# A pre-norm decoder layer with mixture of experts: the first half's order of steps laid out anew

## The reference

```
x = x + attn(ln(x))        # latent attention: down to 32 channels, rotary, causal softmax
                           # within the tile, back to 256
x = x + xattn(ln(x), ctx)  # 32 query heads in 8 groups, head size 8, causal softmax
x = x + ffn(ln(x))         # 32 experts, inner size 96, gated by silu;
                           # the best 8 by softmax, kept until their share reaches 0.8
```

## Time and profile before

| | |
|---|---|
| median of 3 runs | 587.49 us |
| lowest, highest | 585.48, 590.56 us |
| the profiled execution | 586.84 us |
| its span, first to last instruction | 584.1 us |
| TensorE busy | 481.9 us (82%) |
| VectorE busy | 380.1 us (65%) |
| GpSimd busy | 326.2 us (56%) |
| ScalarE busy | 310.5 us (53%) |
| granted TensorE clock, mean | 0.956 |

### The profile page before, as it was taken

One profiled execution on the slowest core, in us unless ns is written; L12 is line 12 of the kernel. 1 busy time (PEld: TensorE's weight loads), 2 busy tenths in 40 slices (PEclk: granted clock), 3 DMA queues, 4 the chain that ended last, 5 costly groups with the idle time before them and its releaser, 6 DMA issues.

```text
span 584.1 us, 12942 instructions
## 1 busy us (share of the span) xinstructions
PE 481.9 (82%) x3248; PEld 401.4 (69%) x3248; DVE 380.1 (65%) x1856; ACT 310.5 (53%) x869; POOL 326.2 (56%) x473
## 2 busy tenths in 40 slices
PE   3689999999999999997588688878888888888750
PEld 2577777777787777776377577777777777778640
DVE  4357888787777778787257344444444446978875
ACT  2477777777777777772424234444444444444430
POOL 4112377766666676765555755555555555655570
PEclk9999999999999999997889879999999999999975
DMA  7422448622223223112643667775544569898665
GB/s 206 130 91 81 145 142 242 182 89 94 92 93 103 92 93 103 66 65 88 189 138 128 218 198 251 238 214 159 148 122 131 159 184 291 296 300 281 203 194 186
DMA packets 52408, 93.82 MB, mean 161 GB/s; under 512 B 9991, under 2 KB 41263, under 8 KB 52147
## 3 DMA queue, kind: packets, MB, share of 16 engines
q1 hardware_dynamic: 37346, 46.11, 27.3%
q0 software_dynamic: 12240, 32.14, 14.8%
q10 hardware_dynamic: 2752, 14.76, 8.0%
HBM read 53.61 MB, written 43.41 MB: 166 GB/s over the span
## 4 chain that ended last, share of the span: by engine, by line
PE 59%; issue 11%; DVE 9%; ACT 9%; another core or an unknown queue 7%; DMA 2%; POOL 1%; ACTq 1%; POOLq 0%; DVEq 0%
PE bank L1387 12%; PE bank L1415 10%; PE bank L1087 6%; PE bank L1254 4%; PE bank L1228 4%; PE bank L1342 3%; DVE NM L776 3%; PE bank L1272 3%; PE bank L1267 3%; ACT VC L491 3%; PE bank L1209 2%; DVE NM L778 2%; PE bank L1405 2%; PE bank L1082 2%
## 5 line engine op out<-in xcount | busy, mean ns | idle before, releaser
L466 POOL DMA_INDIRECT rows<-rowb,idx x112 | 110.8, 989 | 65.7 <-DVE rowb L876 36.0
L1415 PE MATMUL bank<-wd_sb,VC 96*128 x286 | 80.9, 406 | 45.5 <-ACT VC L491 38.9
L1387 PE MATMUL bank<-wgu_sb,PT 128*128 x572 | 108.3, 333 | 5.9 <-issue 5.8
L474 POOL DMA_INDIRECT parts<-PT,dst_all x72 | 71.0, 986 | 68.9 <-ACT PT L491 50.9
L1387 PEld LDWEIGHTS bank<-wgu_sb,PT 128*128 128x128 f32 x572 | 93.6, 194 | 7.1 <-issue 7.1
L1415 PEld LDWEIGHTS bank<-wd_sb,VC 96*128 96x128 f32 x286 | 51.3, 195 | 61.6 <-issue 57.1
L985 DVE SCALAR_TENSOR_TENSOR PT<-PT,bank 128x192 f32<-128x192 f32 x72 | 25.2, 350 | 103.5 <-ACT PT L619 73.4
L491 ACT ACTIVATE PT<-bank 128x512 f32<-128x512 f32 (+1 forms) x108 | 64.1, 595 | 36.5 <-remote 13.7
L619 ACT ACTIVATE PT<-bank 128x192 f32<-128x192 f32 x72 | 24.1, 334 | 97.9 <-PE bank L1387 69.0
L585 ACT ACTIVATE PT<-bank 128x512 f32<-128x512 f32 x96 | 53.7, 621 | 4.7 <-PE bank L1254 4.7
L491 ACT ACTIVATE Q<-bank 9x256 fp32r<-9x256 f32 (+1 forms) x96 | 42.8, 446 | 10.2 <-PE bank L1223 6.4
(11 more groups left out here) (270 smaller groups left out, 1166.1 us busy)
## 6 DMA issues: line engine op xcount, KB each, us to landing
pool_a<-rows SPq DMA_DIRECT2D x96, 148.5 KB
qN<-rows SPq DMA_DIRECT2D x47, 148.5 KB
wgu_sb<-wgu_d SPq DMA_DIRECT2D x8, 768.0 KB
rows<-pad SPq DMA_DIRECT2D x33, 152.0 KB
pool_a<-parts ACTq DMA_DIRECT2D x5, 896.0 KB
KA<-parts ACTq DMA_DIRECT2D x5, 896.0 KB
Q<-parts ACTq DMA_DIRECT2D x4, 896.0 KB
wd_sb<-wd_d SPq DMA_DIRECT2D x2, 1536.0 KB
```

The costliest lines, as they stand in the source:

```text
L466: gp.indirect_dma_start(out=rows, out_offset=bass.IndirectOffsetOnAxis(ap=idx[b % 2][:, k:k + 1], axis=0), in_=rowb[b % 2][:, :], in_offse ...
L474: gp.indirect_dma_start(out=parts, out_offset=bass.IndirectOffsetOnAxis(ap=dst[q % NDST][:, j:j + 1], axis=0), in_=yb[q % FEED][:, j, :], ...
L1387: last = t.matmul(GU_PS[q % 2][:, j * 2 * NI:(j + 1) * 2 * NI], xTb[q % 2][:, j, k * P:(k + 1) * P], wgu_sb[:, k, one_of(expert[i]), :].sq ...
L1415: last = t.matmul(Y_PS[q % 2][:, j * D:(j + 1) * D], hTb[q % 2][:, j, :], wd_sb[:, one_of(expert[2 * q + j]), :].squeeze(1), start=True, s ...
```

## The change

All offsets of the first half are replaced, on all engines, and `mx` gets its wait for `Q2` by halves. Cut to its core:

```diff
 PERIOD = 18.74
 AT = {
...
-    "POOL": {"r1": -12, "r4": -2.2, "r7": 3.9, "r13": 17.4, "kL": 29.5, "r17": 46.3, "wo": 51.5, "xT": 60, "sc0": 74.6, "sc1": 77.4, "sc2": 80.5,
-           "sc3": 82.6, "sc4": 84.5, "sc5": 86.4, "sc6": 87.7},
-    "SP": {"ldx": -6.0, "ldc": -2.0, "n3": 42.5, **{f"w{n}": 25.0 + 12.0 * n for n in range(10)}}}
+    "POOL": {"r1": -4.76, "r4": -3.71, "r7": 9.29, "r13": 18.36, "kL": 31.5, "r17": 47, "xT": 50.53, "wo": 52.71, "sc0": 74.6, "sc1": 77.4,
+           "sc2": 80.5, "sc3": 82.6, "sc4": 84.5, "sc5": 86.4, "sc6": 87.7},
+    "SP": {"ldx": -6, "ldc": -2, "n3": 41.27, **{f"w{n}": 25.0 + 12.0 * n for n in range(10)}}}
...
-PAIR0, PAIR = 47.1, 3.2
...
 END = {
-    "PE": {"oT": 46.9, "wo": 50.1, "xT": 53.3, "lg": 56.5, "rk": 59.7},
-    "ACT": {"oT": 47.3, "xT": 53.6, "g1": 57},
...
-    "POOL": {"r17": 28.5, "wo": 51.3}}
+    "PE": {"oT": 49.29, "wo": 49.66, "xT": 51.34, "lg": 51.56, "rk": 57.28},
+    "ACT": {"oT": 45.1, "xT": 51.2, "g1": 57.99},
...
+    "POOL": {"r17": 28.31, "wo": 47.99}}
...
@@ def mx(u)
                     if u == 0:
                         pe.wait_ge(S["KA"], nth("KA", b))
-                        pe.wait_ge(S["Q2"], nth("Q2", b, 2))
+                    if pair == 0:
+                        pe.wait_ge(S["Q2"], nth("Q2", b, hf + 1))
```

More of the change, by code:

```diff
@@ L51 @@
 AT = {
[3 rows of a table removed]
-           "vt": 43.5, "oT": 46.6, "wo": 50.8, "xT": 56.9, "lg": 58.0, "rk": 62.9, "la1": 74.5 + (SEEN - 1) * PERIOD,
-           "la2": 80 + (SEEN - 1) * PERIOD, "la3": 86.2 + (SEEN - 1) * PERIOD},
[6 rows of a table removed]
-           "po": 62.9, "g7": 64, "g8": 73.7, "g9": 74.2, "g10": 75.2, "g11": 75.4, "g12": 75.6, "g13": 75.8, "la1": 77.4 + (SEEN - 1) * PERIOD,
-           "la2": 83 + (SEEN - 1) * PERIOD, "la3": 86.5 + (SEEN - 1) * PERIOD},
-    "POOL": {"r1": -12, "r4": -2.2, "r7": 3.9, "r13": 17.4, "kL": 29.5, "r17": 46.3, "wo": 51.5, "xT": 60, "sc0": 74.6, "sc1": 77.4, "sc2": 80.5,
-           "sc3": 82.6, "sc4": 84.5, "sc5": 86.4, "sc6": 87.7},
@@ L67 @@
-    "SP": {"ldx": -6.0, "ldc": -2.0, "n3": 42.5, **{f"w{n}": 25.0 + 12.0 * n for n in range(10)}}}
[3 rows of a table added]
+           "pv1": 38.53, "vt": 43.63, "oT": 45.66, "wo": 49.31, "xT": 55.7, "lg": 56.09, "rk": 62.4, "la1": 74.5 + (SEEN - 1) * PERIOD,
+           "la2": 80.0 + (SEEN - 1) * PERIOD, "la3": 86.2 + (SEEN - 1) * PERIOD},
[6 rows of a table added]
+           "g9": 73.62, "g10": 74.22, "g11": 74.82, "g12": 75.08, "g13": 75.1, "la1": 77.4 + (SEEN - 1) * PERIOD, "la2": 83.0 + (SEEN - 1) * PERIOD,
+           "la3": 86.5 + (SEEN - 1) * PERIOD},
@@ L71 @@
 END = {
-    "PE": {"oT": 46.9, "wo": 50.1, "xT": 53.3, "lg": 56.5, "rk": 59.7},
-    "ACT": {"oT": 47.3, "xT": 53.6, "g1": 57},
-    "DVE": {"wo": 50.6, "n3": 52.2, "g1": 56.9, "g2": 57.9, "g3": 58, "g4": 58.1, "g5": 58.2, "po": 60.3, "g6": 61, "g7": 61.1},
-    "POOL": {"r17": 28.5, "wo": 51.3}}
+    "PE": {"oT": 49.29, "wo": 49.66, "xT": 51.34, "lg": 51.56, "rk": 57.28},
+    "ACT": {"oT": 45.1, "xT": 51.2, "g1": 57.99},
+    "DVE": {"wo": 50.21, "n3": 50.91, "g1": 56.18, "g2": 57.58, "g3": 57.81, "g4": 58.03, "g5": 58.69, "g6": 58.84, "po": 59.88, "g7": 60.79},
```

## The result

The changed kernel took 629.14 us (median of 6 runs, 623.51 to 630.05) beside 589.71 us of the kernel before in the same session (6 runs, 585.48 to 590.56): ratio 1.065, 95% interval 1.062 to 1.069. The forecast was 589.0 us, no change. The profiled execution took 630.05 us, with a span of 627.9 us.

A forecast was written before the change was run, and what follows sets the result against it. TensorE, in a loop with the other engines, was taken to bound the first half at 15.87 us a tile. Terms -1.3 - 0.75 + 4.2 - 0.6 = +1.5 us on 586.84, plus 0.65 to the median, gave 589.0 us; range 580 to 594.5.

The forecast's parts named there:

- The part on GpSimd's order: First half, GpSimd: four scatters ahead of r7 make a 16.25 us loop, 0.38 us longer a tile, +4.2 over eleven.
- C: Rival: scatters landing over 3.5 us after their start hold xT, r1, r4, so r5 waits; 594.5 or 604 us; chance 0.08.
- GpSimd's loop (A): Rival: loop through GpSimd, TensorE and VectorE sets the period at 16.25 us; 589.0 us, range 585 to 593; chance 0.50.
- TensorE's order and the split wait: First half: mx0 earlier, waiting only for Q2's first half, r4 ahead of c; 0.25 us a period gained, the wait costing 0.
- the loop's last term: VectorE, from r9's maximum to g13's end: 9.21 us less 0.56 before r5 and about 0.1 for mx0, giving 8.55.
- VectorE's order: r4 ahead of wo removes VectorE's 0.56 us idle before r5 (L682); the other reorderings are worth 0.
- The first tiles: Up to tile 4: -1.3 us once from ScalarE's kT behind r12, and -0.75 for tiles 1 to 3 without scatters.
- The sum: Whole kernel: -1.3 - 0.75 + 4.2 - 0.6 = +1.5 us, giving 589.0 us.
- the end: Last tile: c of tile 15 about 0.6 us earlier, block list about 1 us later; taken -0.6, bounds -3 and +2.

The follow-up runs named there:

- e13: Changed kernel with GpSimd's rope addition r7 moved from behind the fourth scatter to between the second and third: 519.5 us beside 524.9 of before, ratio 0.990.
- e7: The changed kernel unaltered, run again in a session where the kernel before took 525.9 us: 524.7 us, ratio 0.999.
- e3: Changed kernel with TensorE's order of before, every other engine as changed: 537.5 us beside 524.6 of before, ratio 1.022.
- e10: Kernel before with a GpSimd addition and a wait behind each indirect scatter of tiles 12 to 15 and the second half: 690.8 us, ratio 1.314.
- e5: The changed kernel unaltered, run again: 638.6 us beside 597.0 of before, ratio 1.072.
- e15: The kernel of e13 again, where before took 589.6 us: 591.2 us, ratio 1.003.
- e17: The kernel of e13 once more, where before took 589.7 us: 591.3 us, ratio 1.003.
- e16: The kernel of e13 with GpSimd's third scatter of tiles 12 and 13 waiting for pv1 of tiles 14 and 15: 585.3 us beside 589.7, ratio 0.992.
- e18: The kernel of e16 once more: 584.4 us beside 588.9 of before, ratio 0.991.

## Why the prediction was wrong

**What failed.** The part on GpSimd's order costed a row of four scatters by GpSimd's own rows: four slots, 5.24 us, and what waits for the step behind them. What the row does to the engine beside it was taken as nothing and not bounded: `pv0` and `pv1` of TensorE run in just that stretch. In the measured condition that was worth 2.5 to 2.9 us of lateness a tile, about 3.5 us longer tiles with the halved clock behind it, where the sum had 0.38, and 38.6 us in all. No rival had it: the largest, C, ended at 604 us.

**Where it could have been seen.** Tile 15 of before had it in full, and the forecast had the row: 4.55 us before ScalarE's copy at 288.65, "ends on something the profile doesn't name; it can move either way. Taken -0.6, bounds -3 and +2". That wait is the lateness of `pv1` of tile 15, beside which before had a row of scatters too. The change brought it into every tile with scatters, at about half the size. I took a wait without a name as a peculiarity of its place, when the question was what ran beside it and nowhere else.

**A rule for the wrong mechanism.** The forecast weighed the rule of the Trainium skill (SBUF — State Buffer, SBUF: two separate sides) that VectorE's two-port modes lock GpSimd out of its port, which would stretch the scatters and put the kernel over 600 us. The time was over 600 us, but not by that: the four scatters of the changed kernel last 1.05, 0.96, 0.96 and 0.96 us, as the forecast said from the earlier trace rows. GpSimd was not held up; TensorE's semaphores were. No run shows the lockout.

**GpSimd's loop (A).** Right in mechanism and size wherever nothing lies over it: 16.12 us measured (16.25 forecast), 0.39 us a tile above before (0.38), `r8` released by `qk`. e13 takes it away with one number and stands 1% below before. In the measured condition it was hidden: `r8` stood behind `vt`, which waits for the late `pv1`, and in one such tile started 1.8 us behind the end of the rope addition (0.06 us in e7).

**TensorE's order and the split wait.** Their 0.25 us a tile can't be read alone. e13, which has them and not the loop, runs at 15.7 to 16.0 us in all but one tile, beside 15.73 of before: no gain in the steady tiles. But the 8.55 us of the loop's last term needed TensorE's order: in e3 that term is 9.49. The forecast had put what it took off there down to VectorE's order and to `mx0`.

**The first tiles.** Forecast -1.3 - 0.75 = -2.05 us up to tile 4. In the traces of the first session the first `r8` stands at 13.84 us (14.46 before) and that of tile 4 at 74.01 (75.48): -1.5, of which -0.6 was there at the first `r8`. In the 525 condition, e7 against e10: 72.03 and 75.12, -3.1, of which -0.9 (13.27 and 14.21) was there at the first. Sign and order right.

**Landing (C).** In most tiles the token column of e7 waits for the last scatter until 2.5 us behind that scatter's start (157.71 to 160.25), where C needed 3.5. In one tile, the first two rows, it waited until 5.1 us behind it (91.50):

```profile
96.60 0.18 POOL L456 COPY rowb<-cob 128x1 f32<-128x1 f32 x1 [3.51 <-DMA rows<-rowb,idx]
97.89 0.31 DVE L681 TENSOR_SCALAR chat<-bank,mv_lnc,scalars 128x32 f32<-128x32 f32 x1 [1.57 <-POOL scalars L415]
...
157.71 0.96 POOL L465 DMA_INDIRECT rows<-rowb,idx  x1 [0.30 <-issue]
158.66 0.63 POOL L438 CAST KL<-KA 105x512 fp32r<-105x512 f32 x1
160.25 0.18 POOL L456 COPY rowb<-cob 128x1 f32<-128x1 f32 x1 [0.95 <-DMA rows<-rowb,idx]
```

There VectorE's `r5` waits for GpSimd, as C said, and this is the tile of 17.8 us: 1.7 us above the others, where C's rule gives 5.1 - 3.5 = 1.6. So C's mechanism is real, its price per tile right, and it struck once in eleven tiles. In the trace of the changed kernel one landing took 4.4 us and the others up to 3.4. C was rightly unlikely as the rule of every tile.

**The sum.** In the 525 condition +5.5 us in the eleven tiles (forecast +4.2) meet -3.1 at the start (-2.05), and the medians differ by -1.1 us, so some -3.5 is left for the end (-0.6; by difference, not shown). The forecast's "no change" holds there in part by luck: the start and the end gave more than it said, and the tiles took more. In the condition that it was made for, it missed by 40 us. The upper end of the range was also off by its own terms: A with 1.34 us a slot and an end 2 us worse give 589.0 + 1.1 + 2.6 = 592.7 us, not 594.5.

## What to carry to other kernels

When steps are reordered on one engine, ask not only who waits for the moved step, but what now runs beside it on the others; where TensorE's semaphores come late beside a row of indirect DMAs, try a step with a wait of its own between them, or a wait on what runs beside. A long wait that the profile can't name is worth a look at every engine in that stretch before it is called local, since the change may repeat it. And run both kernels in several sessions before a difference of some per cent is read as a property of the code: here the same two programs stood at 0.999 and at 1.065.

## What the hardware showed

- In the 590 condition TensorE's semaphores come late beside rows of GpSimd's indirect DMAs. In the steady tiles of the changed kernel (this trace and e5) `pv1`'s comes 0.8 to 1.0 us behind the end of the fourth; a break behind two of them, or a wait, takes most of that away. Shown by e13's kernel (e15, e17) against the changed one, and by e16 and e18. In tiles 14 and 15 it came from before the row's end (e17) to 1.3 us behind the last (e5), and in three traces over 2 us behind the fourth. Whether it is the arithmetic or only its completion that stands, no run shows, nor whether GpSimd's issuing or the transfers themselves do it.
- It is not a matter of `pv`'s form (four column groups of 32). In the second half of the trace of before, of the TensorE semaphores that can be matched one to one with a matmul ending beside a scatter, 124 of 194 come more than 0.3 us behind it, all of them of transposes and products without such groups; in e7 none of 312. The second half takes 297 us in the changed kernel's first trace and 235 us in e7. That this lateness makes the difference between the two conditions is likely, but no run tried it in the 590 condition.
- In the 525 condition the same instructions under the same scatters are 0.04 us late. What makes the condition is open; chip 3 had both. The traces can be told apart by another sign: those of the 590 condition hold 6900 to 7021 semaphore updates, of which 4080 to 4237 are of DMA landings, those of the 525 condition 11619 to 11975, of which 8337 to 8502. The recording therefore differs with the condition. Every timed run lists a span and a clock, so no run shows whether the late semaphores exist without recording, or are an effect of it; that rival stands.
- Stretches of 1.6 to 3.1 us in which nothing starts on TensorE were followed by a granted clock of 0.50 in eight of twelve late tiles of the changed kernel's first trace and in eight of twelve of e5, mostly for 3.4 us.
